# A decoder layer in one launch: the dt matmuls and the last down tile contract over 128 rows, and all three tables of step orders are replaced

## The reference

```python
# 1: a selective scan
xn = x * rsqrt(mean(x * x) + 1e-6) * norm_scale
hidden, gate = split(xn @ in_w + in_b)              # 256 and 256
h = silu(causal_conv(hidden, 4 taps))
xpj = h @ xproj_w                                   # ts 64, B 16, C 16
delta = softplus(ts @ dt_w + dt_b)                  # dt_w is 64 x 256
state = exp(A * delta_t) * state + delta_t * B_t * h_t     # 16 states of 256 channels
y_t = sum_n(state * C_t) + D * h_t
out = (y * silu(gate)) @ out_w + out_b
# 2: attention, 16 heads of 8, keys and values from ctx, softmax over 64 keys
# 3: 8 experts of width 176, the top 2 weighted by the router, and a shared one of width 176
y = sum_e cw_e * (silu(x @ wg_e) * (x @ wu_e)) @ wd_e + silu(x @ wg_s) * (x @ wu_s) @ wd_s
```

## Time and profile before

| | before |
|---|---|
| median of 3 runs | 1898.13 us (1893.06 to 1901.54) |
| span of the profiled execution | 1896.3 us |
| PE busy (matmuls) | 1679.0 us, 89% |
| DVE busy | 1504.8 us, 79% |
| ACT busy | 1421.6 us, 75% |
| POOL busy | 1548.3 us, 82% |
| mean granted TensorE clock | 0.952 of 2.4 GHz |
| DMA engines | 24% busy |

### The profile page before, as it was taken

How to read it: one execution, slowest core, us unless ns; L and a number is a source line. 1 busy time by engine, 2 the same in 40 slices (tenths; PEclk the granted TensorE clock), 3 DMA queues, 4 the chain that set the end, 5 groups by cost and what they waited for, 6 DMA issues and landing times. The chain is left out here.

```text
span 1896.3 us, 25668 instructions
## 1 busy us (share of the span) xinstructions
PE 1679.0 (89%) x7046; PEld 960.4 (51%) x7046; DVE 1504.8 (79%) x1890; ACT 1421.6 (75%) x4402; POOL 1548.3 (82%) x1284
## 2 busy tenths in 40 slices
PE   4678999999899999989999998999999899998976
PEld 1234454656545465654646565464655545465544
DVE  4888878888897888988788888879888897878332
ACT  5479687786978778797887869788787978767362
POOL 0678888989898888988888898888889898898734
PEclk7679999999999999999999999999999999999988
DMA  2312312222221212322121233212223321231102
GB/s 97 90 39 79 95 49 85 64 68 101 79 95 51 84 62 68 101 79 94 48 89 62 68 101 79 94 49 88 62 68 101 79 95 49 77 96 49 62 3 65
DMA packets 125918, 140.43 MB, mean 74 GB/s; under 512 B 44048, under 2 KB 69456, under 8 KB 125776
## 3 DMA queue, kind: packets, MB, share of 16 engines
q1 hardware_dynamic: 125776, 138.79, 24.4%
HBM read 133.77 MB, written 4.98 MB: 73 GB/s over the span
## 5 line engine op out<-in xcount | busy, mean ns | idle before, releaser
L1171 POOL TENSOR_TENSOR prod<-state,c_rep 128x1024 f32<-128x1024 f32 x256 | 610.0, 2385 | 36.7 <-PE p_y L629 18.7
L1034 DVE TENSOR_TENSOR_SCAN state<-decay,p_drive 128x1024 f32<-128x1024 f32 x256 | 584.6, 2284 | 26.1 <-ACT decay L771 12.8
L771 ACT ACTIVATE decay<-delta,a_neg 128x504 f32<-128x504 f32 x512 | 360.1, 721 | 51.8 <-DVE state L1034 50.5
L629 PE MATMUL p_y<-prod,ident 128*128 128x512 f32 x768 | 397.3, 610 | 0.0
L1024 DVE TENSOR_TENSOR p_drive<-u,p_drive 128x1024 f32<-128x1024 f32 x256 | 312.7, 1221 | 66.7 <-PE p_drive L617 66.4
L903 ACT ACTIVATE ex<-p_ring,nmax 128x64 f32<-128x64 f32 x1024 | 307.4, 368 | 2.9 <-DVE nmax L1086 2.3
L903 ACT ACTIVATION_READ_ACCUMULATOR ex<-p_ring,nmax 128x1 f32 x1024 | 253.7, 262 | 0.0
L729 PE MATMUL p_ring<-x2T,wg 128*128 128x512 f32 x416 | 234.6, 665 | 3.6 <-ACT us L955 3.6
L729 PE MATMUL p_ring<-x2T,wu 128*128 128x512 f32 x384 | 200.8, 621 | 31.8 <-DVE km L1145 19.4
L1224 POOL TENSOR_TENSOR ex<-ex,rden 128x512 f32<-128x512 f32 x128 | 144.9, 1132 | 81.0 <-DVE rden L1090 80.7
L943 ACT ACTIVATE gt<-p_ring 128x512 f32<-128x512 f32 (+1 forms) x208 | 123.8, 596 | 116.3 <-PE p_ring L729 113.1
(11 more groups left out here) (141 smaller groups left out, 3110.5 us busy)
## 6 DMA issues: line engine op xcount, KB each, us to landing
c_rep<-c_rows SPq DMA_DIRECT2D x256, 256.0 KB, 3.6
cwr<-cw_rows SPq DMA_DIRECT2D x64, 256.0 KB, 3.4
ctxT<-in_ctx_t SPq DMA_DIRECT2D x32, 256.0 KB, 5.5
cwr<-cw_rows SPq DMA_DIRECT2D x32, 224.0 KB, 2.9
cwr<-cw_rows SPq DMA_DIRECT2D x32, 192.0 KB, 2.8
cwr<-cw_rows SPq DMA_DIRECT2D x32, 160.0 KB, 3.0
xf<-in_x SPq DMA_DIRECT2D x16, 256.0 KB, 4.4
xb<-in_x SPq DMA_DIRECT2D x16, 256.0 KB, 4.7
```

Of the source, the lines that this page charges most:

```text
L629: pe.matmul(p_y[1 - first][:], ident[:], prod[:, slot_of(c, n), 1 - first, :], start=False, stop=n == STATE - 1, skip_group_check=True).th ...
L771: act.activation(decay[:, n % 2, j, :].rearrange("p (b t) -> p b t", t=SEQ)[:, :, 1:], delta[:, c.parity, j, :].rearrange("p (b t) -> p b ...
L1034: dve.tensor_tensor_scan(state[:, slot_of(c, n), :, :].rearrange("p j t -> p (j t)"), decay[:, n % 2, :, :].rearrange("p j t -> p (j t)"), ...
L1171: pool.tensor_tensor(mine, state[:, slot_of(c, n), :, :], c_rep[:, n % C_SLOTS, :].unsqueeze(1).to_broadcast([128, HALVES, T]), ALU.mult). ...
```

## The change

`wdt` becomes a tile of 128 rows, padded on the host with 64 rows of zeros, and each dt matmul reads all 128 rows of `xp_sb`. The last down tile is read with all 128 rows; rows 48 to 127 of `acts[12]` are set to zero once at the start by DVE. All fifteen lists of the three tables are replaced. The steps in them, their number and their waits are the same; in FIRST_TEXT the text is three lines longer, so lines from there on are numbered 3 higher.

```diff
-        wdt = sb("wdt", [RANK, INNER])
+        wdt = sb("wdt", [128, INNER])
...
-                    mm = pe.matmul(p[:], wdt[:, i * 128:(i + 1) * 128], xp_sb[0:RANK, :], start=True, stop=True)
+                    mm = pe.matmul(p[:], wdt[:, i * 128:(i + 1) * 128], xp_sb[:], start=True, stop=True)
...
-                            rows = slice(0, REST if j == SPLIT else 128)
                             mm = pe.matmul(p[:, g * D:(g + 1) * D],
-                                           acts[j][rows, (2 * i + g) * 128:(2 * i + g + 1) * 128],
-                                           wd[rows, j, :], start=False, stop=j == FFN_TILES - 1)
+                                           acts[j][:, (2 * i + g) * 128:(2 * i + g + 1) * 128],
+                                           wd[:, j, :], start=False, stop=j == FFN_TILES - 1)
...
             dve.memset(vm[:], 0.0)
+            dve.memset(acts[SPLIT], 0.0)
...
-        "w_xproj": xproj, "w_dt": np.asarray(L0_attn_dt_w),
+        "w_xproj": xproj, "w_dt": np.pad(np.asarray(L0_attn_dt_w), ((0, 128 - RANK), (0, 0))),
...
     "pe": (
-        "scan.B_row3 tail.down1 back.q0 scan.B_row4 scan.y_sum2 scan.y_sum3 back.v1 back.score0 "
...
+        "scan.B_row3 tail.down1 scan.B_row4 scan.y_sum2 back.v1 back.q0 scan.B_row5 back.score0 "
...
```

More of the change, by code:

```diff
@@ L80 @@
     "pe": (
[15 rows of a table removed]
-    "act": (
[16 rows of a table removed]
-    "dve": (
[12 rows of a table removed]
-    "pool": (
[7 rows of a table removed]
+        "scan.B_row3 back.q0 back.v1 back.score0 scan.B_row4 scan.y_sum2 back.score1 scan.B_row5 "
+        "back.score2 back.turn0 scan.y_sum3 scan.y_sum4 scan.y_sum5 scan.y_sum6 back.mix0 "
+        "back.score3 back.turn1 scan.B_row6 scan.y_sum7 back.turn2 scan.y_sum8 scan.y_sum9 "
+        "back.score4 scan.B_row7 back.mix1 back.mix2 scan.y_sum10 back.turn3 back.score5 "
+        "scan.y_sum11 scan.B_row8 back.mix3 front.xp0 back.turn4 back.score6 scan.B_row9 "
+        "scan.y_sum12 front.less0 back.score7 front.less1 back.turn5 back.aout0 back.mix4 "
+        "scan.y_sum13 scan.B_row10 back.mix5 scan.y_sum14 back.turn6 scan.B_row11 back.turn7 "
+        "scan.y_sum15 back.mix6 back.x2T0 front.dt0 back.mix7 scan.B_row12 back.aout1 scan.y_sum18 "
+        "front.dt1 back.x2T1 scan.B_row13 scan.y_sum19 back.route0 back.up_g0 back.up_g1 "
+        "scan.B_row14 back.up_u0 scan.y_sum22 back.up_g2 back.up_u1 back.cwT0 front.gate1 "
+        "scan.y_sum23 back.up_u2 back.up_g3 back.up_g4 scan.B_row15 back.up_u3 back.up_g5 "
+        "scan.y_sum26 scan.y_sum27 back.up_u4 back.up_g6 back.up_u5 back.up_u6 back.up_g7 back.up_u7 "
+        "scan.y_sum28 back.up_g8 back.up_g9 back.up_u8 back.up_g10 front.B_row0 back.up_u9 "
+        "scan.y_sum29 scan.y_sum30 back.up_g11 head.xnT0 head.xnT1 back.up_u10 front.B_row1 "
+        "scan.y_sum31 head.hid0 back.up_g12 scan.k0 tail.down1 back.up_u11 head.hid1 scan.v0 "
+        "scan.mout0 front.B_row2 scan.mout1 head.gate0 back.down0 scan.x1T0 scan.x1T1"),
+    "act": (
[16 rows of a table added]
+    "dve": (
[12 rows of a table added]
+    "pool": (
[7 rows of a table added]
     "sp": (
[4 rows of a table removed]
[4 rows of a table added]
 }
@@ L154 @@
-        "scan.B_row15 back.up_u4 scan.y_sum23 back.up_g5 scan.y_sum26 back.up_u5 back.up_g6 "
-        "back.up_g7 back.up_u6 back.up_u7 back.up_g8 scan.y_sum27 back.up_g9 front.B_row0 back.up_u8 "
-        "head.xnT0 back.up_g10 back.up_u9 back.up_g11 head.xnT1 scan.y_sum28 back.up_u10 front.B_row1 "
-        "scan.y_sum29 head.hid0 scan.y_sum30 back.up_u11 scan.y_sum31 back.up_g12 front.B_row2 "
-        "scan.k0 head.hid1 scan.v0 scan.mout0 scan.mout1 head.gate0 back.down0 scan.x1T0 scan.x1T1"),
@@ new lines @@
+        "scan.y_sum12 back.mix3 back.score7 back.turn5 scan.B_row10 back.aout0 back.mix4 "
+        "scan.y_sum13 back.turn6 back.mix5 scan.y_sum14 back.turn7 back.mix6 scan.B_row11 "
+        "scan.y_sum15 back.mix7 back.aout1 scan.B_row12 back.x2T0 scan.y_sum18 front.gate1 "
+        "scan.y_sum19 back.x2T1 scan.B_row13 back.route0 front.dt0 front.dt1 back.up_u0 back.up_g0 "
+        "back.up_g1 scan.B_row14 scan.y_sum22 back.up_g2 back.up_u1 scan.y_sum23 back.cwT0 "
+        "back.up_g3 back.up_u2 back.up_u3 scan.y_sum26 scan.y_sum27 scan.B_row15 back.up_u4 "
@@ new lines @@
+        "back.up_g4 back.up_g5 back.up_u5 back.up_g6 back.up_g7 back.up_u6 back.up_u7 back.up_u8 "
+        "back.up_g8 back.up_g9 head.xnT0 scan.y_sum28 scan.y_sum29 front.B_row0 head.xnT1 "
+        "back.up_g10 back.up_u9 head.hid0 back.up_g11 back.up_u10 back.up_u11 scan.y_sum30 "
+        "front.B_row1 back.up_g12 scan.y_sum31 head.hid1 scan.k0 scan.v0 scan.mout0 scan.mout1 "
+        "head.gate0 front.B_row2 back.down0 scan.x1T0 scan.x1T1"),
+    "act": (
[15 rows of a table added]
+    "dve": (
+        "tail.up_g6 tail.up_g7 scan.gated_h0 tail.up_u6 back.scan15 tail.up_g8 tail.up_g9 "
+        "scan.drive0 tail.up_g10 tail.up_u9 scan.scan0 tail.up_g11 back.gated0 scan.drive1 "
+        "back.gated1 tail.up_u11 tail.up_g12 scan.scan1 back.stats0 front.taps0 back.stats1 "
+        "front.taps1 scan.drive2 scan.scan2 front.taps2 front.silu0 tail.stats4 scan.drive3 "
+        "scan.scan3 tail.stats5 scan.drive4 scan.scan4 front.taps3 back.score0 scan.drive5 "
+        "back.score1 back.sum0 scan.scan5 back.score2 back.sum1 front.silu1 back.score3 scan.drive6 "
+        "back.sum2 scan.scan6 back.score4 scan.drive7 back.sum3 scan.scan7 back.score5 back.sum4 "
+        "scan.drive8 scan.scan8 back.score6 back.sum5 scan.drive9 scan.scan9 scan.gated_h1 "
+        "back.score7 back.sum6 back.stats2 scan.drive10 back.sum7 scan.scan10 scan.drive11 "
+        "scan.scan11 back.stats3 scan.drive12 scan.scan12 scan.drive13 back.route0 scan.scan13 "
+        "back.r_rank0 back.up_g0 back.up_u0 back.up_g1 back.r_cw0 scan.drive14 back.up_g2 "
+        "scan.scan14 back.up_g3 back.up_u3 front.delta0 back.up_g4 back.up_g5 back.up_u5 "
+        "scan.drive15"),
```

25 lines of the change are left out of this document (4 added, 21 removed), and 251 rows, old and new, of tables (FIRST_TEXT, LAST_TEXT, ORDER_TEXT).

## The result

The changed kernel takes **1971.6 us** (median of 4 runs, 1969.35 to 1973.45) where the kernel before takes 1897.7 on the same chip: a ratio of 1.039, 95% interval [1.037, 1.041]. It is 74 us slower. Forecast were 1854 us and a range up to 1880, with a chance of 0.05 for slower: the prediction was wrong.

A forecast was written before the change was run, and what follows sets the result against it. No engine stood far apart (PE busy 89%), but PE was taken as the one waited for around down and dt. 23 + 14 + 7 = 44 us off the 1896.3 us span gave 1852.3, as median 1854; range 1834 to 1880.

The forecast's parts named there:

- Part 1: PE's dt and down matmuls: without switching between 64 or 48 rows and 128, 1.9 us a turn, 23 us saved.
- Part 2: PE's clock in the middle turns: half of its falls around dt go, saving 14 us (0 to 28).
- the rival by which they stay in every turn: PE's clock around dt: falls remain in every turn since rows do not count, 0 instead of 14, 1868 us; chance 0.15.
- Part 3: Outside the middle turns, fill and drain: 7 us saved, with 6 from rows, 2 from new orders, 0.5 lost to zeroing.
- Part 4: New step order in the middle turns: mostly moves cover, counted at 0 us, ends -12 and +12.
- The sum: Whole kernel: 23 + 14 + 7 = 44 us saved, giving 1854 us.
- The one for slower: POOL's gu7 ahead of prod15: a late ACT copy for tile 7 delays prod15, 1910 us at 5 us late; chance 0.05.
- POOL did not become the bound: Down stretch: rival that POOL becomes the bound, rows worth 7 instead of 23 us, 1870 or 1880 us; chance 0.12.
- The other rivals: Whole kernel: all clock falls go, 1840 us, chance 0.18; or nothing PE waits for changes, 1896 +- 5, chance 0.08.
- the signs for being wrong: Middle turns: a fall in every turn, longer PE wait at mout or first score, or turns over 110 us.

The follow-up runs named there:

- experiment 1: The kernel before with its three old tables of step orders, plus only the 128 rows of dt and down: 1855.1 us, ratio 0.976.
- experiment 7: Changed kernel, middle turns, with gu1 ahead of prod13 again on POOL and silu0, silu1 back behind sum1, sum3 on DVE: 1914.9 us.
- experiments 3 and 4: Changed kernel with only the middle table as before: 1893.4 us; changed kernel with only the first and last tables as before: 1958.3 us.
- Experiment 13: Probe behind the last step of experiment 1's kernel: four kinds of DVE step with POOL idle, beside POOL products, beside POOL memsets; 1909.8 us.
- experiment 9: Kernel of experiment 1 with gu1 behind prod13 on POOL in middle turns, and prod13 held until DVE has made r_cw: 1855.0 us.

## Why the prediction was wrong, point by point

**Part 1 (the rows) had the cost right and its share of the time too high.** The second group of down in the changed kernel, and dt:

```profile
1060.01 1.95 PE L750 MATMUL p_ring<-wd,km 128*128 128x128 f32 x16
1061.79 1.28 PE L750 MATMUL p_ring<-wd,acts_more 128*128 128x128 f32 x10
1062.91 0.39 PE L742 MATMUL p_ring<-x,ident 128*128 128x128 f32 x2
1063.13 1.61 PE L750 MATMUL p_ring<-wd,km 128*128 128x128 f32 x13
...
1012.36 1.96 PE L668 MATMUL p_ring<-xp_sb,wdt 128*128 128x512 f32 x4
1014.16 1.02 PE L732 MATMUL p_ring<-x2T,wu 128*128 128x512 f32 x2
```

Ten instructions in 1.12 us (1.40 before), the pair behind them 0.22 (0.32), the group 3.12 against 3.51; four dt matmuls in 1.80 us with nothing behind them. That is 0.38 a group, to the digit. The Trainium skill, page "TensorEngine Tiling (Array Packing)", section "Key Properties", states that changing the tiling mode drains TensorE; the 0.38 us fit that, but no run here shows a drain as such. What reached the time was less than the 1.9 us a turn that I took. In experiment 1 the 12 turns take 1296.7 us, 31.0 less than before, where parts 1 and 2 had 23 + 14 = 37. Turns with one fall of 3.4 us can be compared: 110.0 us before, 108.7 now. So the rows gave 1.3 us a turn, 16 us in all and not 23; it lies between the ends of 7 and 23.

**Part 2 (half of the falls) was right with the old order.** In experiment 1 the clock falls to 1.2 GHz in six of the twelve middle turns, each time within 0.9 us of the start of dt, 20.5 us in all against 58.0 before. A turn with a fall is 1.3 us longer than one without, and the falls make up the other 15 of the 31 us, where 14 had been forecast. So the rival by which they stay in every turn is ruled out for the old order. With the new order part 2 was not right: there the clock falls 19 times in these turns, 64.8 us in all, for 3.4 us each time and at changing places: four times within 0.9 us of the start of dt, five times some 12 us behind it, four times some 30 and six times 64 to 70. One of those some 30 us behind it, at 1042.6, comes behind a new wait of PE for ACT's `us`, the one that is late by `cwT`:

```profile
1041.36 0.44 PE L654 MATMUL p_ring<-ident,xn 128*128 128x128 f32 x2 [2.17 <-ACT us L957]
```

Held against the kernel before, falls are no cause of the loss: 64.8 against 58.0 us at half speed are 3.4 us of matmuls. Held against the rows alone they may carry part of it: 44.3 us more at half speed hold back up to 22 us of matmuls, of the 85.5 us by which the twelve turns are longer. They became fewer where the waits of DVE were taken away (8 in experiment 7), but no run keeps the order and removes the falls alone.

**Part 3 (the outside) failed for its orders.** With the rows alone the fill was 299.4 us instead of 303.7 and the drain 257.8 instead of 264.9, 11 us gained where I had 5 without orders. The new outer tables then cost 38 or 13 us (experiments 3 and 4), where I had counted them at a gain of 2, between -6 and +10.

**Part 4 is the step that failed.** The prediction says: "I count the order at **0**, ends -12 and +12 (1 us a turn, about the waits of one engine on another at one of these places)". The middle table cost 103 us beside the old outer tables, and the middle turns are 7.1 us longer than in experiment 1 (115.2 - 108.1). The error was in what I asked of each moved step: whether its input would be there and who waits for its output. I didn't ask what it would run beside. The move of `gu1` behind prod13, which cost 21 to 35 us, I didn't mention. The other place I took for a gain: "in the new list POOL does both its first products before that layer norm". That is what brought 5.1 us of unbroken products beside DVE's taps and `silu`.

The evidence was in the trace of before: `delta`, a step with two SBUF operands, took 2.32 us in the mean and 1.2 at the shortest, `r_prob` 0.98 and 0.19, the taps 0.91 where POOL was busy and 0.75 where it was idle. I read none of these spreads. The Trainium skill has the rule too, page "SBUF — State Buffer", section "Who interferes with whom": a DVE instruction with two SBUF inputs contends with a GpSimd instruction that reads SBUF, not with one that only writes. Experiment 13 agrees with it in each part. I didn't hold it against the lists.

**The sum.** 44 us were forecast as gain; the rows alone gave 46 (1900.8 - 1855.1), so without the new tables the forecast of 1854 would have stood. In part that would have been luck: the rows gave 16 in place of 23 in the middle turns, and fill and drain 11 in place of 5.

**The rivals.** The one for slower named `gu7` ahead of prod15 and a late copy; in the changed kernel POOL has no wait ahead of `gu7` in any of the twelve turns, and the loss came from other products and another mechanism, so its 0.05 was no foresight. POOL did not become the bound either: it is busy 97.9 of 115.2 us a turn. The other rivals didn't occur. Of the signs for being wrong, middle turns over 110 us came true.

**What stays open.** Two places give back 51 to 57 of the 78 us that the old middle table gives back. For the other 21 to 27 the taps (1.04 us in experiment 7 against 0.86 in experiment 1) and `gated_h` (1.31 against 0.75) are still long in these runs, which is the same kind of wait, but no run took theirs away, and the new lists of PE, ACT and the DMA queue were not tried by themselves. Why the new outer tables lose is open.

## What to carry to other kernels

When steps are reordered, check each engine's new neighbours as well as its dependencies: a DVE step with two SBUF operands beside a POOL step that reads SBUF costs the rest of that POOL step, and a 32-column step that heads a chain is hurt as much as a wide one. The wait shows as busy time of DVE and not as idle time, so compare the mean of a group with its shortest step. Holding the POOL step back until a short DVE step on the path is done was worth 35 us here, though the held step came later; and measure a new order apart from the change of instructions that comes with it, because here the one hid a gain of 46 us behind a loss of 117. Of all that was run, 128 rows with the old tables (1855.1 us) is the best, and experiment 9 is like it (1855.0).
